# Four transformer blocks with cross-attention on one core: TensorE's steps woven in pairs, and GpSimd waiting inside each stack

## The chip, the core and the metric

The kernel runs on one NeuronCore of a Trainium2 chip. The engines are TensorE (PE: matmuls and their weight loads, PEld), VectorE (DVE), ScalarE (ACT), GpSimd (POOL) and SyncE (SP, which here issues DMAs). The metric is the device time of one launch in microseconds (us).

## The reference, cut to what matters

A batch of 4 sequences, 256 tokens by 128 features, goes through four blocks. With `heads` splitting 128 features into 16 heads of 8:

```python
def attend(q, k, v):
    w = softmax(einsum('bhqd,bhkd->bhqk', heads(q), heads(k)) / sqrt(8))
    return einsum('bhqk,bhkd->bhqd', w, heads(v))
...
x = x + gate * (attend(q, k, v of modulate(ln(x))) @ W + b)
x = x + attend(q of ln(x), k, v of ln(context)) @ W + b
x = x + gate * mlp(modulate(ln(x)))
```

Blocks 0 and 1 are self-attention, cross-attention and a GELU MLP; block 2 is one cross-attention with modulated norms; block 3 is a self-attention in shifted windows of 64 tokens, a cross-attention in which each query keeps only its 16 highest scores per head, and a SwiGLU MLP. That makes seven attentions (l = 0 to 6; l = 5 is "window", l = 6 is "topk", the others "full") and three MLPs (l = 7, 8, 9), in the order 0, 1, 7, 2, 3, 8, 4, 5, 6, 9 for each of the 4 batches.

## The kernel before

**Steps and their order.** The work is cut into steps (kind, batch b, layer l, number u). Each engine runs its own fixed list, `ORDERS[engine]`, worked out before the launch by `plan` (line 623). `plan` is a list scheduler: it places the ready step with the highest rank first. A rank is the length of the tail of work behind the step plus priorities from tables (`LEAD`, `BIAS`, `EXTRA`). `BUSY` holds the planner's durations, `SLOTS` the buffers: 8 PSUM banks, 2 slots of key and query parts, 3 of weights. The four batches are independent chains, and the lists interleave them. At run time engines wait for semaphores, each in its own order.

**One attention.** VectorE takes mean and variance (`stats`), GpSimd centres x (`z`: lines 1168 to 1172, the first of which negates the mean), TensorE transposes it (`normed`, L1505), ScalarE copies it with the modulation. TensorE projects keys and queries (L1517, L1518). ScalarE and GpSimd split them into high and low parts (`k_parts`, `qk`; L1278, L1281, L1187). GpSimd then issues four DMAs (`stack`, u = 0 to 3, L1158), each of which lays one plane of 4 heads into `qk_stack`, 32 partitions for each head. A plane is 256 KB. Nothing but these DMAs goes through GpSimd's DMA queue.

**Scores and weights.** A step of `scores` or `weights` (u = 0 to 7) covers two heads of plane u // 2, in row groups 0 and 1 of TensorE where u is even and 2 and 3 where it is odd. For the full kind it is four matmuls with 32 rows and 256 columns, two tiles of 128 queries by two heads, into two banks:

```python
for t in range(NT):
    for j in range(2):
        g = 2 * (u % 2) + j
        ins = nc.tensor.matmul(ps[:, j, at:at + (P if window else N)], ...
```

VectorE reduces the scores to row maxima (L1406). TensorE transposes these (L1554), ScalarE copies them, and SyncE lays them into the stack by an 8 KB DMA (`maxima`, L1120, "qk_stack<-centred" in the trace). Then the `weights` steps repeat the product transposed (L1566), ScalarE takes the exponential (L1298), and `mix` multiplies by the values (L1590). The topk layer has 16 steps of one head each (L1544). For each one VectorE runs two passes that find the 16 highest (L1416 to L1429), and GpSimd turns the rest into a mask (L1227), which TensorE adds (L1577).

**What the planner assumes.** A step of scores or weights costs TensorE 0.46 us, and 0.22 less right behind a step in the other row groups (`beside`). A `stack` step costs GpSimd 1.0 us. Its data move 1.9 us later, or when the queue is free, for 1.25 us. A row DMA lands 2.2 us after its issue, whatever else is in flight. Where TensorE is expected to stand idle, spare matmuls on the identity are put in (L1473).

**Start.** GpSimd waits for the key rows (`k_rows_s`, line 1151) ahead of its whole list. They are a constant of the stack that ScalarE's queue loads.

Of the kernel before, what the change touches and what calls it, by code (L numbers as in the profile page):

```python
# [141 lines left out]
def scores_of(l):  # L142
# [8 lines left out]
    ("dve", "stats"): 0.68, ("pool", "z"): 2.0, ("pe", "normed"): 0.36, ("act", "normed"): 0.45,  # L151
    ("pe", "qk"): 1.0, ("act", "k_parts"): 0.94, ("act", "qk"): 0.95, ("pool", "k_parts"): 0.77, ("pool", "qk"): 0.77, ("sp", "load"): 0.6, ("pool", "stack"): 1.0,
# [22 lines left out]
TO_QUEUE, STACK_TIME, LANDS, AHEAD = 1.9, 1.25, 0.6, 1.75  # L175
HOP = 0.13
SLOTS = {"bank": 8, "qk": 2, "pt": 3, "picks": 2, "gd": 2}
# [12 lines left out]
    ("act", "context", 0, 1): -13.2, ("act", "context", 0, 2): 4.2, ("act", "context", 0, 6): -9.8,  # L190
    ("act", "context", 0, 8): -1.0, ("act", "context", 0, 9): -3.6, ("act", "context", 1, 0): -5.2,
    ("act", "context", 1, 1): -13.1, ("act", "context", 1, 5): -0.7, ("act", "context", 1, 8): 0.1,
    ("act", "context", 2, 0): -40.0, ("act", "context", 2, 1): 7.3, ("act", "context", 2, 3): -4.9,
    ("act", "context", 2, 4): -13.1, ("act", "context", 2, 5): -8.1, ("act", "context", 2, 7): 4.4,
    ("act", "context", 2, 8): -0.9, ("act", "context", 2, 9): -6.1, ("act", "context", 3, 1): 2.2,
    ("act", "context", 3, 2): 19.7, ("act", "context", 3, 3): -3.5, ("act", "context", 3, 5): -26.8,
    ("act", "context", 3, 6): 0.1, ("act", "context", 3, 7): -100.0, ("act", "context", 3, 9): 66.2,
    ("act", "heads_out", 0, 0): 0.9, ("act", "heads_out", 0, 2): 53.8, ("act", "heads_out", 0, 3): -12.5,
    ("act", "heads_out", 0, 4): -4.9, ("act", "heads_out", 0, 6): -4.8, ("act", "heads_out", 0, 7): -24.5,
    ("act", "heads_out", 0, 9): 28.8, ("act", "heads_out", 1, 3): -14.3, ("act", "heads_out", 1, 4): 3.5,  # L200
    ("act", "heads_out", 1, 5): -3.0, ("act", "heads_out", 1, 9): 34.0, ("act", "heads_out", 2, 1): 1.7,
    ("act", "heads_out", 2, 2): 50.5, ("act", "heads_out", 2, 4): 11.8, ("act", "heads_out", 2, 5): 5.1,
    ("act", "heads_out", 2, 6): 0.9, ("act", "heads_out", 2, 7): -3.6, ("act", "heads_out", 2, 8): -21.0,
    ("act", "heads_out", 2, 9): -0.2, ("act", "heads_out", 3, 1): -17.5, ("act", "heads_out", 3, 2): 58.0,
    ("act", "heads_out", 3, 3): -12.8, ("act", "heads_out", 3, 5): 3.4, ("act", "heads_out", 3, 6): -8.5,
    ("act", "heads_out", 3, 8): 0.9, ("act", "heads_out", 3, 9): -42.0, ("act", "k_parts", 0, 2): 66.7,
    ("act", "k_parts", 0, 4): 1.2, ("act", "k_parts", 0, 5): -29.6, ("act", "k_parts", 0, 7): -7.7,
    ("act", "k_parts", 0, 9): 35.2, ("act", "k_parts", 1, 0): 16.0, ("act", "k_parts", 1, 3): 56.6,
    ("act", "k_parts", 1, 4): -12.3, ("act", "k_parts", 1, 5): 1.0, ("act", "k_parts", 1, 7): 4.9,
# [358 lines left out]
    ("pe", "values"): 0.1, ("pool", "gated"): 0.6, ("pool", "k_parts"): -3.6, ("pool", "pre"): -11.2,  # L568
    ("pool", "qk"): 137.4, ("pool", "stack"): -3.6, ("pool", "topk"): 283.6, ("pool", "z"): -2.3,
    ("sp", "load"): -114.6, ("sp", "maxima"): 115.5, ("sp", "store"): 42.9,  # L570
}


def w_group(blk):
# [48 lines left out]
def plan(lead, landed, table_load=1.3, patience=0.0):  # L623
# [222 lines left out]
    while left:  # L846
# [25 lines left out]
        if beside(t, s):  # L872
            d, lag = d - 0.22, 0.2
# [799 lines left out]
```

## Time and profile before

| | us |
|---|---|
| median of 3 runs | 672.29 |
| lowest and highest | 669.69, 678.34 |
| the profiled execution | 665.29 |
| its span, first to last instruction | 663.5 |
| mean granted clock of TensorE | 0.863 |

In the profiled execution PE is busy 570.0 us (86% of the span), DVE 490.9 (74%), ACT 386.3 (58%), POOL 306.4 (46%). A busy time says how long an engine had an instruction in it, not that it set the pace: that is read from the windows and the waits. In rows of lines, "L12" is line 12 of the kernel, the text is output<-inputs, x is the count, and behind the bar stand busy us and mean ns, then the idle time ahead of the instructions and who ended it. Granted clock 1.0 is full speed.

### The profile page before, as it was taken

Reading aid. Unit: us, or ns where it says so; the run is one execution under the profiler, and the core shown is the slowest. Engines: PE = TensorE matmul, PEld = TensorE weight load, DVE = VectorE, ACT = ScalarE, POOL = GpSimd, SP = SyncE. Lnnn points to the kernel's source line nnn. Section 1 sums busy time; section 2 is a strip of 40 time slices with the busy share of each in tenths; the row PEclk is TensorE's granted clock in tenths of the full one; section 3 lists DMA queues with packets and bytes.
Section 4 is the critical chain, followed back from the end, with each engine's and each line's share of the span. In section 5 each row is a group of like instructions: output and inputs, shape, how many; then the busy total and the mean of one; then the engine's idle time right before and its main releaser. Section 6 shows DMA issues by size and latency. Waiting matters only on the chain.

```text
span 663.5 us, 14489 instructions
## 1 busy us (share of the span) xinstructions
PE 570.0 (86%) x5152; PEld 378.9 (57%) x5152; DVE 490.9 (74%) x1291; ACT 386.3 (58%) x669; POOL 306.4 (46%) x584
## 2 busy tenths in 40 slices
PE   3888989899999999999998889786999987867477
PEld 3645556566756565657665556554655664634246
DVE  2577767853859687745377727999999999999953
ACT  2546878799696887886757766452233531611133
POOL 6884535435845444364562446641341446111133
PEclk9858999999999999998989979777575795765779
DMA  9560344302333533020335043140020002000000
GB/s 319 143 159 3 88 106 112 73 2 54 76 67 69 105 77 78 2 65 2 66 72 123 2 129 68 28 101 0 2 65 2 2 10 64 9 1 2 1 2 16
DMA packets 15062, 39.23 MB, mean 59 GB/s; under 512 B 2641, under 2 KB 6801, under 8 KB 14737
## 3 DMA queue, kind: packets, MB, share of 16 engines
q0 software_dynamic: 8960, 29.37, 20.1%
q1 hardware_dynamic: 5312, 8.46, 3.8%
q8 instruction: 43, 0.70, 0.4%
q10 hardware_dynamic: 720, 0.49, 0.3%
q14 instruction: 27, 0.21, 0.1%
HBM read 7.96 MB, written 0.52 MB: 13 GB/s over the span
## 4 chain that ended last, share of the span: by engine, by line
DVE 38%; PE 37%; ACT 8%; DMA 6%; issue 6%; POOL 4%; ACTq 0%; POOLq 0%
PE psum L1590 10%; DVE left L1419 8%; DVE left L1429 7%; DVE top L1426 6%; DVE top L1416 6%; DVE maxima L1406 5%; PE psum L1566 5%; PE psum L1536 5%; ACT softmax_T L1298 4%; DMA qk_stack<-centred 3%; PE psum L1625 3%; PE psum L1636 3%; DMA qk_stack<-qk_parts 2%; DVE maxima L1402 2%; PE psum L1617 2%
## 5 line engine op out<-in xcount | busy, mean ns | idle before, releaser
L1298 ACT ACTIVATE softmax_T<-psum 128x1024 f32<-128x1024 f32 (+1 forms) x224 | 210.9, 962 | 111.7 <-PE psum L1577 73.3
L1406 DVE TENSOR_REDUCE maxima<-psum 128x4 f32<-128x1024 f32 x160 | 190.1, 1216 | 52.4 <-PE psum L1536 51.6
L1566 PE MATMUL psum<-qk_stack 32*128 32x256 f32 (+1 forms) x896 | 114.9, 346 | 28.1 <-DMA qk_stack<-centred 9.6
L1590 PE MATMUL psum<-softmax_T,values 128*32 128x256 f32 (+1 forms) x1792 | 129.9, 408 | 4.8 <-ACT softmax_T L1298 3.5
L1566 PEld LDWEIGHTS psum<-qk_stack 32*128 32x128 f32 x896 | 72.3, 202 | 71.0 <-issue 31.0
L1227 POOL TENSOR_SCALAR unpicked<-left 128x512 bf16<-128x512 f32 x64 | 39.5, 616 | 136.0 <-DVE left L1429 135.3
L1536 PE MATMUL psum<-qk_stack 32*128 32x256 f32 (+1 forms) x768 | 89.6, 335 | 9.2 <-ACT softmax_T L1298 2.4
L1536 PEld LDWEIGHTS psum<-qk_stack 32*128 32x128 f32 x768 | 58.9, 200 | 37.5 <-issue 16.5
L1590 PEld LDWEIGHTS psum<-softmax_T,values 128*32 128x32 f32 x1792 | 56.7, 118 | 40.3 <-issue 12.0
L1187 POOL TENSOR_TENSOR qk_parts<-qk_parts 128x256 fp32r<-128x256 f32 x56 | 40.9, 730 | 77.0 <-ACT qk_parts L1281 76.6
L1158 POOL DMA_DIRECT2D qk_stack<-qk_parts x112 | 63.7, 580 | 7.0 <-POOL qk_parts L1187 6.3
L1306 ACT ACTIVATE centred<-psum 8x256 f32<-8x256 f32 (+1 forms) x64 | 23.1, 364 | 56.3 <-PE psum L1551 40.9
L1278 ACT ACTIVATE qk_parts<-psum,column_biases 128x512 fp32r<-128x512 f32 x56 | 38.5, 687 | 24.0 <-PE psum L1518 21.0
L1419 DVE MATCH_REPLACE8 left<-top,psum 128x256 f32<-128x256 f32 x128 | 52.0, 414 | 0.0
L1429 DVE MATCH_REPLACE8 left<-top,left 128x256 f32<-128x256 f32 x128 | 51.4, 408 | 0.0
L1416 DVE MAX8 top<-psum 128x8 f32<-128x256 f32 x128 | 48.1, 417 | 2.0 <-PE psum L1544 2.0
L1426 DVE MAX8 top<-left 128x8 f32<-128x256 f32 x128 | 47.9, 416 | 1.3
L1448 DVE TENSOR_TENSOR x<-x,psum 128x256 f32<-128x256 f32 x40 | 16.6, 414 | 41.2 <-PE psum L1636 22.9
L1473 PE MATMUL psum<-identity 128*128 128x256 bf16 x150 | 27.4, 332 | 19.4 <-DVE left L1419 11.5
L1310 ACT ACTIVATE mixed_T<-psum 128x256 f32<-128x256 f32 x56 | 21.5, 385 | 31.9 <-PE psum L1590 31.3
L1172 POOL TENSOR_SCALAR centred<-x,neg_mean,rstd 128x128 f32<-128x128 f32 x80 | 35.2, 447 | 4.4
L1168 POOL TENSOR_SCALAR neg_mean<-mean_var 128x2 f32<-128x2 f32 x48 | 9.4, 196 | 58.6 <-DVE mean_var L1394 44.1
(99 smaller groups left out, 870.3 us busy)
## 6 DMA issues: line engine op xcount, KB each, us to landing
qk_stack<-qk_parts POOLq DMA_DIRECT2D x112, 256.0 KB, 5.1
weights<-in_w SPq DMA_DIRECT2D x1, 1408.0 KB, 13.5
row_biases<-in_rows SPq DMA_DIRECT2D x1, 1088.0 KB, 10.8
weights<-in_w SPq DMA_DIRECT2D x2, 512.0 KB, 5.9
weights<-in_w SPq DMA_DIRECT2D x1, 832.0 KB, 9.0
qk_stack<-centred SPq DMA_DIRECT2D x48, 8.0 KB
weights<-in_w SPq DMA_DIRECT2D x1, 768.0 KB, 4.3
weights<-in_w SPq DMA_DIRECT2D x1, 576.0 KB, 3.7
```

The lines of the kernel that those rows point to most:

```text
L1158: pool.dma_start(QKS[b][:, u, :, :].bitcast(F32), parts[32 * u:32 * u + 32, slot, :, :, :].bitcast(F32)).then_inc(stacked[b][u], 16)
L1187: nc.gpsimd.tensor_tensor(lo, lo.bitcast(F32), parts[:, slot, 0, c, :].bitcast(F32), ALU.subtract).then_inc(done[kind, "pool"], 1)
L1227: nc.gpsimd.tensor_scalar(unpicked[:, n, :, :], left[:, k, :, :], 1.0 / GONE, 1.0, ALU.mult, ALU.add).then_inc(done[kind, "pool"], 1)
L1298: nc.scalar.activation(pT[:, slot, u % 2, :, 0:cols].rearrange("p (i t) n -> p i t n", t=NT), two_banks(step).rearrange("p i (t n) -> p i ...
L1406: nc.vector.tensor_reduce(rows[:, u // 4, u // 2 % 2, g:g + 2, :], ps.rearrange("p i (t k) -> p i t k", t=NT), AX_X, ALU.max).then_inc(fin, 1)
L1416: ins = nc.vector.max(top8[:, b, r, g, t, :], misc[:, N * t:N * t + N])
L1419: ins = nc.vector.match_replace(left[:, k, t, :], top8[:, b, r, g, t, :], misc[:, N * t:N * t + N], -GONE)
L1426: ins = nc.vector.max(top8[:, b, 2, g, t, :], left[:, k, t, :])
L1429: ins = nc.vector.match_replace(left[:, k, t, :], top8[:, b, 2, g, t, :], left[:, k, t, :], -GONE)
L1536: ins = nc.tensor.matmul(ps[:, j, at:at + (P if window else N)], QKS[b][32 * g:32 * g + 32, s, 0, P * t:P * t + P], QKS[b][32 * g:32 * g + ...
L1566: ins = nc.tensor.matmul(ps[:, i, t, 0:P if window else N], QKS[b][32 * g:32 * g + 32, s, 1, P * t:P * t + P], QKS[b][32 * g:32 * g + 32, ...
L1590: ins = nc.tensor.matmul(misc[32 * g:32 * g + 32, queries], V[:, b, t, first:first + 32], pT[:, slot, g // 2, 2 * (g % 2) + t, 0:P if wind ...
```

## The change

It has five parts. TensorE's list may hold woven pairs: two steps of scores, weights (but not those of topk) or topk whose row groups differ. Both sets of waits come first, and then the first tile of A, the first of B, the second of A and the second of B are issued. The planner forms a pair where the second step can start within 0.15 us of the first, and prices it at 0.44 us. `BUSY` has 1.9 for `z` and 0.62 for `stack` in place of 2.0 and 1.0, row DMAs are priced by what is in the queue ahead of them, the scores and weights of odd u need no longer follow those of the even u before, x and context are assumed to land 0.8 and 1.2 us later, and `EXTRA`, `BIAS` and `LEAD` hold other numbers throughout, so all orders differ. GpSimd waits for the key rows only ahead of the first stack. The negated mean is dropped; the mean is subtracted in place. And GpSimd issues plane 2 of a stack only when plane 0 has landed, and plane 3 only when plane 1 has; the planner has no term for this wait.

```diff
-    ("dve", "stats"): 0.68, ("pool", "z"): 2.0, ("pe", "normed"): 0.36, ("act", "normed"): 0.45,
+    ("dve", "stats"): 0.68, ("pool", "z"): 1.9, ("pe", "normed"): 0.36, ("act", "normed"): 0.45,
...
+ROWS_WAY, ROWS_BEHIND = 1.5, 3.0
...
+WOVEN, WOVEN_BESIDE, WOVEN_FIRST, WOVEN_SECOND, WOVEN_SLOWER, TOGETHER = 0.44, 0.1, 0.42, 0.43, 1.67, 0.15
...
+def weaves(step):
+
+    kind, b, l, u = step
+    if kind == "topk":
+        return True
+    return kind == "scores" and ATTN[l]["kind"] == "full" or kind == "weights" and ATTN[l]["kind"] != "topk"
...
-                t = task("pe", ("weights", b, l, u), maxed[u // 2], prev and ("pe", ("weights", b, l, u - 1)),
+                t = task("pe", ("weights", b, l, u), maxed[u // 2], ("pe", ("weights", b, l, u - 1)) if u and (u % 2 == 0 or topk) else None,
...
+        if eng == "pe" and weaves(step):
+            others = [(rank(n), c[0], n) for n in ready["pe"] if (c := choose(n)) is not None]
+            fit = [o for o in others if weaves(o[2][1]) and not groups(o[2]) & groups(t) and o[1] <= s + TOGETHER]
+            if fit:
+                r, at, other = max(fit, key=lambda o: o[0])
+                if any(r + BESIDE < o[0] for o in others if o not in fit and o[1] <= s + 0.3):
+                    other = None
...
+        if other is not None:
+            s = max(s, at)
+            d = WOVEN - (WOVEN_BESIDE if beside(t, s) else 0.0)
...
+            woven[step] = other[1]
...
-            land = end + TO_QUEUE + 0.3
...
+            land = end + ROWS_WAY + min(max(0.0, queue - end - 0.64), ROWS_BEHIND)
...
+ORDERS, SLOT, HAD, TIMES, SPARE, WOVEN_WITH = plan(LEAD, landed)
...
-            pool.wait_ge(k_rows_s, 16 * SLOTS["qk"])
+            first_stack = next(i for i, s in enumerate(ORDERS["pool"]) if s[0] == "stack")
             for step in ORDERS["pool"]:
                 kind, b, l, u = step
                 if kind == "stack":
                     slot = SLOT["qk", ("k_parts", b, l, 0)][0]
+                    if step == ORDERS["pool"][first_stack]:
+                        pool.wait_ge(k_rows_s, 16 * SLOTS["qk"])
+                    if u > 1:
+                        pool.wait_ge(stacked[b][u - 2], 16 * (l + 1))
...
-                    nc.gpsimd.tensor_scalar(nmean[:, b, c, :], mv[:, b, c, :, 0], -1.0, 0.0, ALU.mult, ALU.add)
...
-                        ins = nc.gpsimd.tensor_scalar(dst[:, b, t, :], src[:, b, t, :], nmean[:, b, c, t:t + 1],
-                                                      rstd[:, b, c, t:t + 1], ALU.add, ALU.mult)
+                        ins = nc.gpsimd.tensor_scalar(dst[:, b, t, :], src[:, b, t, :], mv[:, b, c, t, 0:1],
+                                                      rstd[:, b, c, t:t + 1], ALU.subtract, ALU.mult)
...
+            def half(step, t):
...
+                s, ps = u // 2, two_banks(step)
+                own, other = (1, 0) if kind == "weights" else (0, 1)
+                moving = slice(P * t, P * t + P) if ATTN[l]["kind"] == "window" else slice(0, N)
+                for j in range(2):
+                    g = 2 * (u % 2) + j
+                    ins = nc.tensor.matmul(ps[:, j, t * N:t * N + moving.stop - moving.start],
+                                           QKS[b][32 * g:32 * g + 32, s, own, P * t:P * t + P],
+                                           QKS[b][32 * g:32 * g + 32, s, other, moving], start=True, stop=True)
+                return ins
...
+                if weaves(step):
+                    inputs_in(step)
+                    if step in WOVEN_WITH:
+                        other = WOVEN_WITH[step]
+                        banks_free(pe, other)
+                        inputs_in(other)
+                        half(step, 0)
+                        half(other, 0)
+                        half(step, 1).then_inc(fin, 1)
+                        half(other, 1).then_inc(done[other[0], "pe"], 1)
+                    else:
+                        half(step, 0)
+                        half(step, 1).then_inc(fin, 1)
```

## Rows read from the trace of the kernel before

**Rows 1.** The page, busy tenths in 40 slices of 16.6 us.

```profile
PE   3888989899999999999998889786999987867477
DVE  2577767853859687745377727999999999999953
```

**Rows 2.** Windows: length, busy us (count) of PE, PEld, DVE, ACT, POOL, then clock.

```profile
20.00:60.00 40.00, 33.51 (x251) 20.89 (x250) 27.65 (x46) 18.82 (x38) 29.33 (x59) 0.66 0.49 120
60.00:400.00 340.00, 317.38 (x3286) 209.28 (x3288) 223.27 (x362) 266.15 (x452) 171.00 (x330) 0.97 0.30 67
400.00:640.00 240.00, 191.25 (x1458) 126.81 (x1459) 227.25 (x839) 85.83 (x151) 83.72 (x149) 0.72 0.11 25
```

**Rows 3.** Groups of lines, 400 to 640 us: busy us, mean ns, idle before.

```profile
L1419 DVE MATCH_REPLACE8 left<-top,psum 128x256 f32<-128x256 f32 x128 | 52.0, 414 | 0.0
...
L1426 DVE MAX8 top<-left 128x8 f32<-128x256 f32 x128 | 47.9, 416 | 1.3
```

**Rows 4.** Timeline of PE: start us, length us; two places.

```profile
101.95 0.50 PE L1566 MATMUL psum<-qk_stack 32*128 32x256 f32 x4
102.38 0.44 PE L1505 MATMUL psum<-identity,context_centred 128*128 128x128 f32 x2
...
106.44 0.39 PE L1566 MATMUL psum<-qk_stack 32*128 32x256 f32 x2
106.48 0.39 PE L1536 MATMUL psum<-qk_stack 32*128 32x256 f32 x2
106.67 0.28 PE L1566 MATMUL psum<-qk_stack 32*128 32x256 f32 x2
106.68 0.30 PE L1536 MATMUL psum<-qk_stack 32*128 32x256 f32 x2
```

**Rows 5.** Windows of the tile qk_stack alone, PE first.

```profile
60.00:400.00 340.00, 118.12 (x1258) 76.81 (x1260) 42.92 (x76) 0.97 0.30 67
```

**Rows 6.** Groups of lines, 60 to 400 us, DVE and ACT.

```profile
L1406 DVE TENSOR_REDUCE maxima<-psum 128x4 f32<-128x1024 f32 x141 | 167.9, 1216 | 43.2 <-PE psum L1536 42.4
L1298 ACT ACTIVATE softmax_T<-psum 128x1024 f32<-128x1024 f32 (+1 forms) x159 | 155.3, 1001 | 20.7 <-PE psum L1566 19.1
```

**Rows 7.** Timeline of DVE and of POOL in the first 10 us.

```profile
6.67 0.25 DVE L1394 BATCH_NORM_AGGREGATE mean_var<-stats 128x2 f32<-128x6 f32 x2
...
9.48 0.19 POOL L1168 TENSOR_SCALAR neg_mean<-mean_var 128x2 f32<-128x2 f32 x1 [3.07 <-DMA qk_parts<-in_k_rows]
```

**Rows 8.** Groups of lines of POOL, whole span.

```profile
L1158 POOL DMA_DIRECT2D qk_stack<-qk_parts x112 | 63.7, 580 | 7.0 <-POOL qk_parts L1187 6.3 <-issue 0.4
L1168 POOL TENSOR_SCALAR neg_mean<-mean_var 128x2 f32<-128x2 f32 x48 | 9.4, 196 | 58.6 <-DVE mean_var L1394 44.1 <-PE psum L1505 11.1 <-DMA qk_parts<-in_k_rows 3.1
```

**Rows 9.** The chain of work near 80 us, and the list of waits.

```profile
79.96 4.84 DMA qk_stack<-centred
...
PE psum L1566 <- DMA qk_stack<-centred: 9.6, 9, 2.2
PE psum L1505 <- POOL centred L1172: 4.6, 6, 1.6
```

**Rows 10.** Timeline of POOL from 214 us, and of PE at 220 us.

```profile
214.18 2.25 POOL L1158 DMA_DIRECT2D qk_stack<-qk_parts  x4
216.41 0.25 POOL L1168 TENSOR_SCALAR neg_mean<-mean_var 128x2 f32<-128x2 f32 x1
217.84 0.88 POOL L1172 TENSOR_SCALAR centred<-x,neg_mean,rstd 128x128 f32<-128x128 f32 x2
...
220.40 0.44 PE L1505 MATMUL psum<-identity,centred 128*128 128x128 f32 x2 [0.28 <-DVE maxima L1406]
```

**Rows 11.** DMA issues, median us to landing, around 160.2, 156.1 and 215.8 us.

```profile
qk_stack<-qk_parts POOLq DMA_DIRECT2D x1, 256.0 KB, 3.4
...
qk_stack<-qk_parts POOLq DMA_DIRECT2D x2, 256.0 KB, 4.0
...
qk_stack<-qk_parts POOLq DMA_DIRECT2D x2, 256.0 KB, 5.9
```

More of the change, by code:

```diff
@@ L195 @@
[L195 to L204, printed above, removed]
@@ L782, in plan @@
     lists = {e: [] for e in engines}
-    clock, spare = Clock(), {}
+    clock, spare, woven = Clock(), {}, {}
     table, last, queue = "exp", 0, 16.0
@@ L843, in choose, with hold, landing @@
         return s, taken
+    def hold(t, taken):
+        for ring, which in taken:
+            slots[ring] = [o for o in slots[ring] if o not in which]
+            slot[ring, t[1]] = [k for _, k, _ in which]
+            had[ring, t[1]] = sorted({before for _, _, before in which if before is not None})
+    def landing(t, land, end):
+        for r, taker in gives(t):
+            slots[r] += [(land + HOP, k, taker) for k in slot[r, taker]]
+            slots[r].sort()
+        for n in users[t]:
+            waiting[n] -= 1
+            ready_at[n] = max(ready_at[n], land + (HOP if n[0] != t[0] or land > end else 0.02))
+            if not waiting[n]:
+                ready[n[0]].append(n)
     left = len(order)
@@ L880, in plan @@
                 table = fn
-        if eng == "pe" and taken:
-            since = max([free["pe"], IDENTITY_THERE] + [when for _, which in taken for when, _, _ in which])
-            if s - since >= IDLE:
-                clock.until(since)
-                spare[step] = int(min(0.85 * (s - since), 0.3 + 0.6 * (s - since)) * (1.0 if clock.rate == 1 else 1 / 1.8) / SPARE_D)
-                if spare[step]:
-                    clock.run(since, spare[step] * SPARE_D, spare[step] * SPARE_CELLS, 1.8)
         end = clock.run(s, d, cells(step), SLOWER.get(kind, 1.8)) if eng == "pe" else s + d
@@ L891, in plan @@
         lists[eng].append(step)
-        for ring, which in taken:
-            slots[ring] = [o for o in slots[ring] if o not in which]
-            slot[ring, step] = [k for _, k, _ in which]
-            had[ring, step] = sorted({before for _, _, before in which if before is not None})
         land = end + lag
@@ new lines, in _ @@
+                    pe.wait_ge(consts_s, 3)
+                    for i in range(2):
+                        after(pe, "pool", ("topk", b, l, 2 * u + i))
+                        for t in range(NT):
+                            for r in range(NT):
+                                ins = nc.tensor.matmul(ps[:, i, t, P * r:P * r + P],
+                                                       unpicked[:, 4 * SLOT["picks", ("topk", b, l, 4 * s)][0] + 2 * (u % 2) + i, r, P * t:P * t + P], drop[:],
+                                                       start=False, stop=(t == 1 and r == 1))
```

526 lines of the change are left out of this document (276 added, 250 removed), and 339 rows, old and new, of tables (EXTRA, LEAD).

## Prediction

> **What bounds the kernel now.** I read the 40 slices of the page first, then the same span in a few windows. The slices [rows 1] show two stages. From slice 4 to slice 24 TensorE stands at 8 or 9 tenths and VectorE at 5 to 8; from slice 25 on VectorE stands at 9 and TensorE falls. The windows [rows 2] put numbers on that. From 60 to 400 us TensorE is busy 317.4 of 340 us (93%), ScalarE 266.2 (78%), VectorE 223.3 (66%), GpSimd 171.0 (50%), at a clock of 0.97. From 400 to 640 us VectorE is busy 227.3 of 240 us (95%), TensorE 191.3 with a clock of 0.72. The groups of lines name VectorE's work there: four lines of the top-16 passes, 128 instructions each, between 47.9 and 52.0 us a line [rows 3], some 200 us together. None of it falls in the first stage, so the kernel is TensorE's for 340 us and then VectorE's for 240 us, and a microsecond saved in the first stage arrives whole only if the second stage starts earlier by it. The start, 20 to 60 us, is a third case: TensorE at 33.5 of 40 us with a clock of 0.66, GpSimd at 29.3 of 40 (73%) [rows 2].
>
> The diff does five things: it weaves pairs of steps on TensorE, it lets the planner know of that (and gives it other priorities), it lets GpSimd begin before the key rows have landed, it drops one small GpSimd instruction of each norm, and it makes GpSimd wait in the middle of each stack.
>
> **1. Weaving.** A lone step of scores or weights is four matmuls, two row groups by two tiles. It starts at 101.95 and the next step starts at 102.38 [rows 4]: 0.43 us. The change issues the first tile of A, the first tile of B, the second of A, the second of B. What does the kernel before do when two such steps stand next to each other? The four rows at 106.44 [rows 4] answer: two matmuls of L1566, two of L1536, two of L1566, two of L1536, starts 106.44, 106.48, 106.67, 106.68, the last one over at 106.98. The program has all of L1566's step ahead of L1536's, and yet the trace shows them woven already, at 0.54 us for both where a lone one takes 0.50. So for a pair that is adjacent and ready the new program order gives nothing: my value is 0 for these. What can give is the planner: it now prices a pair at 0.44 us in place of about 0.70, and so puts more steps side by side.
>
> The Trainium skill ("TensorE: Matmul & The Clock Gate", section The mechanism) says that matmuls of different row groups start and end in strict program order, without reordering. By that rule a pair in the kernel before would run end to end, and weaving in the program would save the second switch of weights in each. The rows at 106.44 differ from it, and the measurement decides; what it would give is one of the rivals below.
>
> How much can more pairs give? From 60 to 400 us the matmuls that read the stack keep TensorE busy 118.1 us, 1258 of them [rows 5], which is 315 steps of four at 0.375 us each (some are paired now). If every step were half of a pair at 0.43 us for two, that would be 315 x 0.215 = 68 us, so 50 us less; if no further pair forms, 0. Those are the bounds: -50 and 0. Between them I go by the readers. A pair takes four of the eight banks, and the readers need 1.216 us on VectorE and 1.001 us on ScalarE for each step [rows 6], two to three times what TensorE needs to fill it. ScalarE is already at 266 of 340 us, and every shortening pushes it up: at 50 us less it would stand at 266 of 290 (92%). Four free banks at one time, with both inputs landed within 0.15 us of each other, is not the common case. I take a quarter of the room, -13 us. The second stage adds nothing: its matmuls of this kind lie beside a VectorE that is 95% busy.
>
> The Trainium skill ("TensorEngine Tiling (Array Packing)", section PSUM Bottleneck) states that tiling speeds up TensorE but not the emptying of PSUM, which can become the bottleneck. The two rows of the readers agree with it, and it is why I stay far from the upper bound.
>
> **2. The start.** GpSimd's first instruction of the first norm starts at 9.48 after 3.07 us of waiting for the key rows [rows 7]; nothing of the norm reads them. The wait moves to the first stack, at 20 us, when they are long there. Mean and variance of the first batch are there at 6.92 [rows 7], 2.5 us before that norm starts, all four first norms follow one another on GpSimd, and the first stack follows them, so I take -2.5 us (bounds -3.1 and 0; next late would be the weights of the first projection).
>
> **3. The dropped negation.** L1168, 48 instructions of 196 ns, 9.4 us of GpSimd [rows 8]. It lies on the way from statistics to the norm's transpose, but TensorE waits for the centred tile only 4.6 us in the whole span [rows 9]. So 48 x 0.2 us is the upper bound of the gain, 4.6 is the one that waits show, and I take -2. The subtraction in place of an addition keeps the operation's shape, and I give it no other price.
>
> **4. The wait inside a stack.** Today the four planes are issued in a row, 2.25 us [rows 10], 112 issues at 580 ns [rows 8]. A plane with nothing ahead of it lands 3.4 us after its issue, two in a row 4.0 (the median of both), the last two of four 5.9 [rows 11]. With the change plane 2 is issued when plane 0 has landed: some 3.6 us after the first issue, where it was 1.1. It then has little ahead of it and lands at about 3.6 + 3.6 = 7.2 instead of 1.1 + 5.9 = 7.0. Plane 3 waits for plane 1, which lands at about 0.6 + 4.3 = 4.9, and lands at about 4.9 + 3.6 = 8.5 instead of 1.7 + 5.9 = 7.6. (3.6 and 4.3 are my estimates around the 3.4 and 4.0 of the rows.) For the planes themselves I take 0: plane 2 is first read by the fifth step of its attention, four reductions of 1.216 us [rows 6] after the first.
>
> The price is GpSimd's. It is in order, and a stack holds it until plane 3 is out: 4.9 + 0.6 = 5.5 us instead of 2.25, 3.2 us more, 28 times, some 90 us on an engine that is busy 284 us between 20 and 640 us [rows 2]. Queued behind the waiting instruction is whatever GpSimd has next: the norm of another batch, the low parts of its keys and queries, the gated weights, the unpicked masks. TensorE waits for these. The case at 214.18 [rows 10] shows how far the cover goes: the stack ends at 216.43, the norm of another batch starts at 216.41, its centred tile is over at 218.72, and TensorE transposes it at 220.40. It has 1.7 us in hand. 3.2 us later it would be 1.5 us late, and TensorE, in order too, would stand still. That is the upper bound if every stack had such a follower with such a cover: 28 x 1.5 = 42 us; the lower bound is 0, since GpSimd is idle half of the time and a follower may come later. The planner prices a plane at 0.62 us and does not know of the wait, so nothing in the order makes room. I take a quarter, +10 us, because the other three quarters find an idle GpSimd or a slack of more than 3 us.
>
> **5. The row DMAs.** The wait also takes something off: the 8 KB transfer of the maxima runs behind stacks, and in the chain one of them takes 4.84 us [rows 9]. TensorE waits 9.6 us in nine places for it [rows 9]. With at most two planes in flight, and with a planner that prices the queue, I take -3 (bounds -9.6 and 0).
>
> **The sum.** Against the profiled execution, 665.3 us with its 663.5 us span: 665.3 - 13 - 2.5 - 2 - 3 + 10 = 654.8. The median of the runs shown is 672.3, 7.0 above the profiled one, and I carry that over: **661.8 us**, 1.6% less than before. About 2% is what a measurement of this kernel tells from no change.
>
> **The rivals.**
> (a) *The planner finds far more pairs and the wait is hidden.* For it: TensorE is idle only 23 of 340 us, so whatever pairs save there is time, and VectorE has 117 us to spare in that stage. Against it: the readers and the eight banks. With -35 for the pairs and +2 for the wait: 665.3 - 35 - 2.5 - 2 - 3 + 2 = 624.8, and 632 as a median.
> (b) *GpSimd becomes the engine that paces.* The place is the first 60 us and every norm behind a stack. At the start GpSimd is at 29.3 of 40 us [rows 2]; four stacks stand there, and 4 x 3.2 = 12.8 us more is more than the 10.7 us that it has free (40 - 29.3), so the first layers of the later batches slip. If half of the 42 us of point 4 reach TensorE and pairs give 0: 665.3 - 2.5 + 21 = 683.8, 691 as a median. It decides from the point where the wait costs more than the other four give, here 20.5 us; it is slower by 2% when it costs 13 us more than that.
> (c) *Neither works.* Adjacent steps are woven already, no further ones form, the wait falls into GpSimd's idle time: 665.3 - 2.5 = 662.8, 670 as a median.
> (d) *The program's order does what the engine does not.* If most pairs ran end to end today, each would save one switch, 0.215 us; 157 pairs in the first stage make 34 us. That gives 665.3 - 34 - 2.5 - 2 - 3 + 10 = 633.8, 641 as a median. The rows at 106.44 speak against it; I leave it 3%.
>
> **How the numbers follow.** My forecast 40%, (a) 20%, (b) 20%, (c) 17%, (d) 3%. The forecast itself spreads by about 12 us either way, from the quarters that I chose in points 1 and 4. The edge of faster by 2% is at 658.8 and that of slower at 685.7. Faster: (a), (d) and some 15 of the 40 points of the forecast, 0.38. Slower: (b) and a point of the rest, 0.21. Within: 0.41. The range goes from 638, which leaves out half of (a), to 690, which leaves out half of (b).
>
> **What would show it.** Weaving: on TensorE's timeline more groups of eight matmuls of the two lines inside 0.55 us, and from 60 to 400 us fewer busy microseconds for the matmuls of the stack at the same count. If only pairs of the old kind are there, step 1 was wrong. The start: the first negation's place taken by the variance line at about 7 us and the first stack at about 17. The wait: GpSimd's rows of L1158 (at its new line) in groups of two with a gap of 2 to 3 us, the new releaser a plane's DMA, and TensorE's waits for the centred tile and ScalarE's for its key parts. If TensorE's waits for these stay near 5 us, the wait is hidden. The rows: no 8 KB transfer of more than 3 us in the chain. The topk stage would keep its 200 us of VectorE and only begin earlier. What would make me wrong is the order itself: both programs run a fixed order from a planner, and a different set of priorities may place one batch's top-16 work earlier beside TensorE's stage, for which no row of before gives a price.

## The result: 10% slower

| | before | after |
|---|---|---|
| median us | 671.1 | 738.1 |
| lowest and highest | 669.7, 678.3 | 732.9, 744.9 |
| span of the profiled execution | 663.5 | 743.1 |
| mean granted clock of TensorE | 0.863 | 0.814 |

The ratio is 1.101, with a 95% interval of 1.095 to 1.108. The forecast was 661.8 us and its range ended at 690. The executions of one kernel fall into a faster and a slower group; every ratio below compares faster ones alone, every median takes all of them, and the profiled execution of the changed kernel, 6.8 us above its median, is one of the slower ones.

The page of the changed kernel, in the form of [rows 1]; a slice is now 18.6 us:

```profile
PE   4568888799778897889788699659979869787867
...
DVE  2375836673356667473655444668999999999953
```

The windows of [rows 2] again, with one more, because the end is 80 us later:

```profile
20.00:60.00 40.00, 24.54 (x178) 16.25 (x176) 23.25 (x40) 12.40 (x28) 25.89 (x44) 0.66 0.54 120
60.00:400.00 340.00, 290.86 (x2785) 186.76 (x2789) 193.07 (x312) 231.37 (x383) 162.03 (x256) 0.89 0.25 52
400.00:640.00 240.00, 194.74 (x1635) 127.88 (x1627) 190.71 (x619) 103.41 (x197) 99.85 (x166) 0.71 0.21 44
640.00:743.00 103.00, 79.14 (x585) 56.24 (x584) 79.96 (x300) 29.39 (x44) 27.63 (x43) 0.84 0.02 5
```

No engine is full from 60 to 400 us any more. TensorE was busy 317.4 us there with 3286 matmuls [rows 2] and is now busy 290.9 with 2785. ScalarE and VectorE lose 35 and 30 us with it, GpSimd 9. The granted clock of the stage fell too, from 0.97 to 0.89, while TensorE stood idle for 49 us of it and not 23: 64 matmuls of one line (L1625, now L1708) took 394 ns each before and 460 now. What the clock adds to the loss was not told apart. So an engine waits, and the others wait for it. The list of waits names it (engine, waiting line, releaser: us in total, times, longest):

```profile
DVE maxima L1462 <- PE psum L1543: 112.2, 61, 7.9
POOL qk_stack L1215 <- DMA qk_stack<-qk_parts: 99.2, 50, 4.4
...
PE psum L1604 <- POOL centred L1228: 43.5, 27, 4.5
...
PE psum L1604 <- POOL context_centred L1228: 12.6, 3, 7.2
```

GpSimd waits 99.2 us for planes to land, 3.5 us in each of 28 stacks; this wait did not exist before. TensorE waited 4.6 us for centred tiles [rows 9]; it now waits 56.1 us for the two kinds. VectorE's waits for TensorE (112.2 us, and 51.6 before) are the same loss once more, one engine on. One case, on the timeline of GpSimd and then of TensorE (start, length, and in brackets the idle time ahead):

```profile
87.85 1.18 POOL L1215 DMA_DIRECT2D qk_stack<-qk_parts  x2 [0.30 <-POOL qk_parts L1243]
91.73 0.55 POOL L1215 DMA_DIRECT2D qk_stack<-qk_parts  x1 [2.70 <-DMA qk_stack<-qk_parts]
92.90 0.55 POOL L1215 DMA_DIRECT2D qk_stack<-qk_parts  x1 [0.62 <-DMA qk_stack<-qk_parts]
93.52 0.19 POOL L1225 TENSOR_SCALAR var_eps<-mean_var 128x2 f32<-128x2 f32 x1
93.80 0.71 POOL L1226 TENSOR_TENSOR rstd<-var_eps,half_power 128x2 f32<-128x2 f32 x1
94.61 1.58 POOL L1228 TENSOR_SCALAR centred<-x,mean_var,rstd 128x128 f32<-128x128 f32 x2
```

```profile
96.33 0.66 PE L1604 MATMUL psum<-identity,centred 128*128 128x128 f32 x2 [2.03 <-POOL centred L1228]
```

Planes 2 and 3 go out 3.9 and 5.1 us after the first (forecast 3.6 and 4.9). Behind them on the in-order GpSimd stands the norm of another batch, and TensorE stands still 2.03 us for it. Of those 2.03 us, 1.58 - 0.88 = 0.7 come from the norm's last row itself, which took 0.88 us for two tiles before [rows 10]; the dropped negation gives 0.2 of them back. The chain of waits shows the same stretch (start, length, what):

```profile
88.48 4.13 DMA qk_stack<-qk_parts
...
92.90 0.55 POOL qk_stack L1215
...
94.61 1.59 POOL centred L1228 x2
...
96.33 0.66 PE psum L1604 x2
```

The groups of lines of GpSimd give both causes their totals (x count, busy us, mean ns, idle before):

```profile
L1215 POOL DMA_DIRECT2D qk_stack<-qk_parts x112 | 63.6, 568 | 105.9 <-DMA qk_stack<-qk_parts 99.2 <-POOL qk_parts L1243 6.6
L1228 POOL TENSOR_SCALAR centred<-x,mean_var,rstd 128x128 f32<-128x128 f32 x80 | 63.2, 797 | 4.2
```

A centred tile costs 797 ns with the mean subtracted. The added form costs 447 to 454 ns in every kernel below that has it.

### The profile page after: what moved, and what is told of

The parts are those of the page before. It is cut to its first block, busy times and chain, and to the rows that moved or that the text cites. A ratio compares the mean times of both kernels' runs of the same rounds, so it can differ in the third digit from the quotient of the medians.

```text
span 743.1 us, 14558 instructions
## 1 busy us (share of the span) xinstructions
PE 599.1 (81%) x5218; PEld 394.8 (53%) x5218; DVE 491.9 (66%) x1291; ACT 384.6 (52%) x667; POOL 331.4 (45%) x534
## 4 chain that ended last, share of the span: by engine, by line
PE 29%; DVE 23%; POOL 18%; issue 14%; DMA 10%; ACT 5%; POOLq 0%; ACTq 0%; DVEq 0%
DMA qk_stack<-qk_parts 10%; PE psum L1673 7%; POOL centred L1228 5%; PE psum L1543 5%; DVE left L1475 5%; DVE left L1485 5%; DVE top L1482 4%; DVE top L1472 4%; POOL qk_parts L1243 3%; POOL rstd L1226 3%; PE psum L1708 3%; POOL qk_stack L1215 3%; DVE maxima L1462 3%; ACT softmax_T L1354 2%; PE psum L1719 2%
## 5 line engine op out<-in xcount | busy, mean ns | idle before, releaser
L1462 DVE TENSOR_REDUCE maxima<-psum 128x4 f32<-128x1024 f32 x160 | 189.6, 1216 | 112.6 <-PE psum L1543 112.2
L1543 PE MATMUL psum<-qk_stack 32*128 32x256 f32 (+1 forms) x1408 | 137.4, 361 | 17.6 <-ACT softmax_T L1354 9.1
L1673 PE MATMUL psum<-softmax_T,values 128*32 128x256 f32 (+1 forms) x1792 | 138.3, 431 | 5.3 <-ACT softmax_T L1354 4.0
L1543 PEld LDWEIGHTS psum<-qk_stack 32*128 32x128 f32 x1408 | 90.9, 214 | 78.0 <-issue 33.7
L1215 POOL DMA_DIRECT2D qk_stack<-qk_parts x112 | 63.6, 568 | 105.9 <-DMA qk_stack<-qk_parts 99.2
L1673 PEld LDWEIGHTS psum<-softmax_T,values 128*32 128x32 f32 x1792 | 59.5, 124 | 44.8 <-issue 20.0
L1243 POOL TENSOR_TENSOR qk_parts<-qk_parts 128x256 fp32r<-128x256 f32 x56 | 40.7, 729 | 95.2 <-ACT qk_parts L1337 94.9
L1228 POOL TENSOR_SCALAR centred<-x,mean_var,rstd 128x128 f32<-128x128 f32 x80 | 63.2, 797 | 4.2
L1604 PE MATMUL psum<-identity,centred 128*128 128x128 f32 x80 | 19.9, 340 | 44.4 <-POOL centred L1228 43.5
L1559 PE MATMUL psum<-identity 128*128 128x256 bf16 x216 | 37.0, 317 | 12.4 <-DVE cond_silu L1402 6.2
L1504 DVE TENSOR_TENSOR x<-x,psum 128x256 f32<-128x256 f32 x40 | 16.6, 416 | 43.3 <-PE psum L1700 24.2
L1491 DVE RECIPROCAL rden<-psum 128x32 f32<-128x32 f32 x28 | 9.9, 353 | 44.8 <-PE psum L1682 44.7
L1604 PEld LDWEIGHTS psum<-identity,centred 128*128 128x128 f32 x80 | 9.5, 163 | 53.9 <-issue 39.0
```

Source lines behind the costliest of these rows:

```text
L1215: pool.dma_start(QKS[b][:, u, :, :].bitcast(F32), parts[32 * u:32 * u + 32, slot, :, :, :].bitcast(F32)).then_inc(stacked[b][u], 16)
L1228: ins = nc.gpsimd.tensor_scalar(dst[:, b, t, :], src[:, b, t, :], mv[:, b, c, t, 0:1], rstd[:, b, c, t:t + 1], ALU.subtract, ALU.mult)
L1243: nc.gpsimd.tensor_tensor(lo, lo.bitcast(F32), parts[:, slot, 0, c, :].bitcast(F32), ALU.subtract).then_inc(done[kind, "pool"], 1)
L1462: nc.vector.tensor_reduce(rows[:, u // 4, u // 2 % 2, g:g + 2, :], ps.rearrange("p i (t k) -> p i t k", t=NT), AX_X, ALU.max).then_inc(fin, 1)
L1543: ins = nc.tensor.matmul(ps[:, j, t * N:t * N + moving.stop - moving.start], QKS[b][32 * g:32 * g + 32, s, own, P * t:P * t + P], QKS[b][3 ...
L1673: ins = nc.tensor.matmul(misc[32 * g:32 * g + 32, queries], V[:, b, t, first:first + 32], pT[:, slot, g // 2, 2 * (g % 2) + t, 0:P if wind ...
```

## The experiments

The first theory was: the wait costs what its hold of GpSimd costs, and the dropped negation is a loss because the subtraction is slower. Rivals: the new orders are bad by themselves; or the planes are late, and not GpSimd. "The order before" means the old planner numbers, "the new order" the changed ones. Ratios are to the kernel before, run beside, with 95% intervals.

### The parts, one at a time

The wait, alone in the kernel before:

```diff
+                    if u > 1:
+                        pool.wait_ge(stacked[b][u - 2], 16 * (l + 1))
```

> The kernel before with the two waits inside each stack, order and norm of before. Theory H: 671 rises by 25 us or more. My recorded sum gave +10, the half of its upper bound +21. If it rises by 10 or less, the hold costs only in the new order, whose planner prices a plane at 0.62 us in place of 1.0.

> The changed kernel without the two waits inside a stack; all else as changed. Theory H (the hold of GpSimd is the cost: 99 us of waiting on planes in 50 places, with norms and key parts queued behind it): 735 falls by 40 to 65 us, to 670 to 695. Theory N (the norm's subtraction with a column of mean_var is the cost: 797 ns in place of 447, 96 times, 34 us): it falls by less than 25 us. Theory O (the order and the woven pairs are worse by themselves): it stays above 700 whatever is taken away.

The subtraction, alone in the kernel before, and taken back out of the changed one (the reverse of this diff):

```diff
-                    nc.gpsimd.tensor_scalar(nmean[:, b, c, :], mv[:, b, c, :, 0], -1.0, 0.0, ALU.mult, ALU.add)
...
-                        ins = nc.gpsimd.tensor_scalar(dst[:, b, t, :], src[:, b, t, :], nmean[:, b, c, t:t + 1],
-                                                      rstd[:, b, c, t:t + 1], ALU.add, ALU.mult)
+                        ins = nc.gpsimd.tensor_scalar(dst[:, b, t, :], src[:, b, t, :], mv[:, b, c, t, 0:1],
+                                                      rstd[:, b, c, t:t + 1], ALU.subtract, ALU.mult)
```

> The kernel before with the new norm alone (no negation, mean subtracted from mean_var). Each norm on GpSimd gets 0.2 us shorter by the negation and 0.7 longer by two centring instructions at 797 ns. Theory N: 671 rises by 10 us or more. If centring stays at 447 ns here and the time falls by 0 to 3 us, the slow form needs something else of the changed kernel.

> The changed kernel with the norm of before (negated mean in its own tile, added) and with the waits. Theory N: 735 falls by 20 to 34 us, to 701 to 715. Theory H: it falls by 10 us or less. Theory O: it falls by 10 us or less. In each case the centring instructions return to 447 ns if it is their form that makes them slow.

Both parts, in the kernel before; and neither, in the changed one:

> The kernel before with both the waits and the new norm. If the two costs simply add, its rise is the sum of the rises of the two kernels that hold one each; if both draw on the same slack (GpSimd's idle time and the norm's cover of about 1 us), it is more than the sum. If the order is no cause, this kernel reaches the 735 of the changed one within 10 us.

> The changed kernel without the waits and with the norm of before: the new order, the woven pairs and the early start alone. H and N together: 650 to 668, at or a little under before (671), since the pairs form and the start is 2.5 us earlier. Theory O: above 685.

Measured, in us (median; ratio with its interval):

| | order before | new order |
|---|---|---|
| neither | 671.1 (1) | 666.6 (0.993, 0.989 to 0.998) |
| subtraction | 679.9 (1.010, 0.991 to 1.029) | 684.1 (1.022, 1.012 to 1.032) |
| wait | 701.9 (1.048, 1.042 to 1.055) | 719.0 (1.074, 1.066 to 1.082) |
| both | 715.4 (1.067, 1.052 to 1.082) | 738.1 (1.101, 1.095 to 1.108) |

So the new order by itself is not the loss: without the two GpSimd parts it is 0.7% faster than the kernel before. In it the wait costs 719.0 - 666.6 = 52 us and the subtraction 17.5; together that is 70, and both measured 71.5. In the order before the wait costs 31 us and the subtraction 7 us by its ratio, 9 by the medians (its interval reaches below 0). TensorE's waits for centred tiles follow. They stand here for the order before with the wait, for the new order with the wait, then for the new order with neither:

```profile
POOL qk_stack L1160 <- DMA qk_stack<-qk_parts: 97.4, 45, 4.1
...
PE psum L1507 <- POOL centred L1174: 14.9, 14, 3.1
...
PE psum L1538 <- DMA qk_stack<-qk_parts: 10.4, 4, 4.1
...
PE psum L1568 <- DMA qk_stack<-centred: 3.5, 6, 0.8
```

```profile
PE psum L1606 <- POOL centred L1230: 28.1, 16, 4.2
...
PE psum L1606 <- POOL context_centred L1230: 10.4, 3, 6.9
```

```profile
PE psum L1604 <- POOL centred L1228: 3.1, 6, 1.0
...
PE psum L1653 <- DMA qk_stack<-centred: 1.0, 3, 0.4
```

The hold is as long in either order (97.4 and 98.6 us of waiting); what differs is how much of it reaches TensorE: 17.4 us of waits for centred tiles of both kinds in the order before (2.5 of them for the context's) and 38.5 in the new one. The difference, 21 us, is as large as that of the two prices. In the order before TensorE also waits 10.4 us for planes themselves, in four places, all in the window attention; in the kernel before it was 2.0.

### Is it the operation or the place of its operand?

The changed line differs in two things: it subtracts, and it reads the mean from the strided tile of statistics. The first kernel copies the mean, not negated, to its own tile and subtracts it; the second negates it where it is and adds it:

```diff
-                    nc.gpsimd.tensor_scalar(nmean[:, b, c, :], mv[:, b, c, :, 0], -1.0, 0.0, ALU.mult, ALU.add)
+                    nc.gpsimd.tensor_scalar(nmean[:, b, c, :], mv[:, b, c, :, 0], 1.0, 0.0, ALU.mult, ALU.add)
...
-                                                      rstd[:, b, c, t:t + 1], ALU.add, ALU.mult)
+                                                      rstd[:, b, c, t:t + 1], ALU.subtract, ALU.mult)
```

> The kernel before with the mean copied unnegated to its own tile and subtracted there: tells the operation from the operand's place. If the subtraction makes centring slow, its line stands at 797 ns here; if the column of mean_var does, at 447. Time: 671 to 674 at 447 ns, like the new norm plus 0.2 us each at 797.

```diff
-                    nc.gpsimd.tensor_scalar(nmean[:, b, c, :], mv[:, b, c, :, 0], -1.0, 0.0, ALU.mult, ALU.add)
+                    nc.gpsimd.tensor_scalar(mv[:, b, c, :, 0], mv[:, b, c, :, 0], -1.0, 0.0, ALU.mult, ALU.add)
...
-                        ins = nc.gpsimd.tensor_scalar(dst[:, b, t, :], src[:, b, t, :], nmean[:, b, c, t:t + 1],
+                        ins = nc.gpsimd.tensor_scalar(dst[:, b, t, :], src[:, b, t, :], mv[:, b, c, t, 0:1],
```

> The kernel before with the mean negated in place in mean_var and added from there: the other half of the same question. If the place makes centring slow, 797 ns here; if the subtraction does, 447 ns and a time like before.

The second one changes the computation in one place: the two norms of a batch's context share their statistics, so the later one meets a mean that was negated twice. The amount of work is the same. Subtracting from its own tile, and then adding from the statistics (groups of lines):

```profile
L1172 POOL TENSOR_SCALAR centred<-x,neg_mean,rstd 128x128 f32<-128x128 f32 x80 | 63.2, 795 | 4.4
```

```profile
L1171 POOL TENSOR_SCALAR centred<-x,mean_var,rstd 128x128 f32<-128x128 f32 x80 | 35.2, 447 | 4.4
```

It is the operation. The place costs nothing in the instruction's own time. The times go with it: 679.0 us (1.018, 1.001 to 1.036, two runs) and 669.4 (1.004, 0.997 to 1.011).

### GpSimd's time or late planes?

The wait does two things: it holds GpSimd, and it lets planes 2 and 3 land later. One pair of kernels holds GpSimd with the planes on time, by clears of a scratch tile behind every fourth plane (7 or 12 clears, linked one to the next):

```diff
+                    n_planes[0] += 1
+                    if n_planes[0] % 4 == 0:
+                        for _ in range(12):
+                            link(nc.gpsimd.memset(scratch[:], 0.0))
```

> The kernel before without any wait on planes, but with seven linked clears of a scratch tile (about 0.45 us each, 3.2 us) on GpSimd behind each fourth plane. The planes are issued and land as before; only GpSimd is taken for as long as by the hold. Theory Q (the price is GpSimd's queue: norms and key parts stand behind it): +25 to +35 us, as with the waits (+31). Theory L (the price is that planes 2 and 3 land later): +5 us or less.

> As the run with seven clears, which measured 0.26 us a clear with its link and so took GpSimd for only 1.85 us a stack (+11), but with twelve of them, 3.2 us, the length of the hold. Planes are issued and land as before. Theory Q (GpSimd's queue is the price): +22 to +35 us. Theory L (planes 2 and 3 late): it stays at +11 or below +15.

> The new order with the old norm and no wait (666.6 us), with 12 clears of a scratch tile on GpSimd behind every fourth plane, about 3.2 us per stack, planes on time. In the old order the same clears cost +27 us and the wait +31. If the wait's price is GpSimd's time and the new order has less slack on GpSimd, the clears cost more here: +40 to +52 us, 707 to 719 us. If the extra 21 us of the new order come from the late planes (the planner has their readers earlier), the clears cost about +27 us as before, 694 us.

The other kernels let the planes be late with GpSimd free: SyncE issues planes 2 and 3, with the same wait or, as its own comparison, without it:

```diff
+                if kind == "stack":
+                    slot = SLOT["qk", ("k_parts", b, l, 0)][0]
+                    sp.wait_ge(stacked[b][u - 2], 16 * (l + 1))
...
+                if kind == "stack" and u > 1:
+                    continue
```

> The kernel before with planes 2 and 3 issued by SyncE, each with the same wait for the plane two places ahead; GpSimd issues only planes 0 and 1 and waits for none. Planes land as late as in the kernel with the waits. Theory Q: within 8 us of before, or below it, since GpSimd gets 1.1 us a stack back. Theory L: +20 us or more. A price of its own: the rows of the maxima stand behind the waiting plane on SyncE, up to 3.6 us, in the places where a stack and a row meet.

> As the gated one on SyncE, without the waits on planes. GpSimd is freed of 56 issues, 32 us, and nothing is late. Theory Q: -2 to -10 us against before. Theory L: 0 (nothing is later than before).

> The new order with the norm of before, no wait on planes, and planes 2 and 3 issued by SyncE. The new order without the waits stands at 0.993 of before. Theory Q: 0.975 to 0.99. If SyncE's rows suffer behind 256 KB planes, 1.0 or above.

> The new order with the old norm, planes 2 and 3 issued by SyncE with the same wait, GpSimd free; without the wait the same kernel took 672.2 us. If the late planes cost nothing by themselves: 672 to 678 us. If they make up the new order's extra price: about 21 us more, 690 us and above.

| | order before | new order |
|---|---|---|
| 7 clears a stack | 681.5 | |
| 12 clears a stack | 700.0 | 700.1 (1.057, 1.045 to 1.068) |
| planes by SyncE, no wait | 668.7 (1.001, 0.994 to 1.007) | 672.2 (1.003, 0.998 to 1.007) |
| planes by SyncE, wait | 674.9 (1.004, 0.998 to 1.009) | 671.9 (1.012, 1.005 to 1.020) |

The runs of the two kernels without a ratio lie too far apart for one (665.4 to 686.6, and 687.5 to 706.2); beside them before had medians of 670.7 and 672.9. The lowest run of each had a granted clock of 0.858 and 0.851, and beside runs of before at nearly that clock, 668 and 669 us, they make nothing for 7 clears (665.4) and 19 us for 12 (687.5). So by the two ways of reading it 7 clears cost between nothing and 11 us, and 12 clears 19 to 27. The 12 clears in the order before, in groups and in waits:

```profile
L1165 POOL MEMSET scratch<- 128x128 f32 x336 | 70.0, 208 | 17.8
```

```profile
PE psum L1511 <- POOL centred L1178: 17.6, 13, 3.1
```

The clears take (70.0 + 17.8) / 28 = 3.1 us a stack, near the hold's 3.5, and with every plane on time they cost 19 to 27 us where the wait costs 31; TensorE's waits for centred tiles are 17.6 us, with the wait 14.9. With late planes and a free GpSimd these waits are 4.0 us, those for planes 0.7, and the time is above its comparison by 6 us in the one order and not at all in the other (by the ratios 2 and 7 us). So most of the price is that of GpSimd's queue. Whether it grows in proportion to the time held, 51.2 us with 7 clears and 87.8 with 12, can't be told from these runs.

The new order pays more for the same clears: 700.1 - 666.6 = 34 us (by the ratios 6.4%, or 43 us). That is not all of its 52. I expected 707 to 719 us had it been, and 694 had the order made no difference; 700.1 lies between. Late planes alone don't make up the rest (671.9 beside 672.2; by the ratios 1%, with intervals that touch). Between 4 and 18 us of the wait in the new order stay open. They too arrive as late norms: TensorE waits 38.5 us for centred tiles of both kinds with the wait and 27.3 with the clears.

### Is it the start?

Rival (b) laid the loss first on the 20 to 60 us window. The wait only for the first layer, and the key rows' wait alone moved to the first stack:

```diff
+                    if u > 1 and l == 0:
+                        pool.wait_ge(stacked[b][u - 2], 16 * (l + 1))
```

> The kernel before with the waits in the first layer's four stacks only, 4 of 28. If the price is per stack, 31 x 4/28 = 4 us. If it sits at the start, where GpSimd is 73% busy and four stacks follow one another, as my rival (b) put it, 10 us or more.

```diff
-            pool.wait_ge(k_rows_s, 16 * SLOTS["qk"])
...
+                    if step == ORDERS["pool"][first_stack]:
+                        pool.wait_ge(k_rows_s, 16 * SLOTS["qk"])
```

> The kernel before with the wait for the key rows moved ahead of the first stack, nothing else. My recorded term is -2.5 us. If weights or another arrival take its place, 0; GpSimd's first norm then starts near 7 us all the same.

The wait in the first layer alone costs nothing: 670.4 us (1.001, 0.997 to 1.004), with 11.6 us of waiting in six places. The moved wait gives 670.9 us (0.996, 0.992 to 1.001): the first norm starts at 7.62 us instead of 9.48 [rows 7] and the first stack at 18.67 instead of 19.97. That can't be told from no gain.

The wait in the first layer alone was run in the order before only, and the traces show that the new order is different there. Its list for GpSimd has the first norm of a context right behind the second stack, and its list for TensorE has the transpose early: at 27.93 us without the wait, where the kernel before has it at 34.60. With the wait (the new order, the norm of before) it comes at 32.67, after the longest wait of the whole kernel for a centred tile:

```profile
32.67 0.66 PE L1606 MATMUL psum<-identity,context_centred 128*128 128x128 f32 x2 [6.90 <-POOL context_centred L1230]
```

The window of 20 to 60 us, first of the new order with neither part and then with the wait, in the form of [rows 2]:

```profile
20.00:60.00 40.00, 34.74 (x265) 22.32 (x263) 29.15 (x50) 19.41 (x37) 32.86 (x71) 0.66 0.46 117
```

```profile
20.00:60.00 40.00, 26.19 (x191) 17.20 (x193) 24.52 (x42) 14.59 (x30) 26.59 (x55) 0.65 0.51 117
```

TensorE has 8.6 us less of its work done there; in the order before the wait takes 0.8 (33.5 to 32.7). So about 8 of the 21 us by which the new order pays more for the wait lie at the start, if none of them is made up later.

### Does the program's order of a pair matter?

The new order without wait and subtraction, its pairs issued one step after the other:

```diff
                         half(step, 0)
-                        half(other, 0)
                         half(step, 1).then_inc(fin, 1)
+                        half(other, 0)
                         half(other, 1).then_inc(done[other[0], "pe"], 1)
```

> The new order without the waits and with the norm of before, and each of the 69 pairs issued as the kernel before issues two neighbours: all four matmuls of A, then all four of B (both sets of waits still first). Theory R (the engine or its queue weaves neighbours of different row groups by itself, as the rows at 106.44 suggest): the same time as with woven issue, 0.993 of before within 0.5%, and pairs of lines still alternate in the trace. Theory P (program order counts): 69 pairs at 0.2 us, up to 14 us more, 1.01 or above.

665.8 us (0.993, 0.989 to 0.997), and woven 666.6 (0.993). A pair in TensorE's timeline of the unwoven kernel:

```profile
106.49 0.51 PE L1543 MATMUL psum<-qk_stack 32*128 32x256 f32 x8
```

Eight matmuls in 0.51 us, with the program's order A, A, B, B; both steps have one line here, so the rows show the time of a pair and not who alternates. The matmuls of the stack alone, from 60 to 400 us, first of the woven and then of the unwoven kernel, in the form of [rows 5]:

```profile
60.00:400.00 340.00, 108.85 (x1198) 70.67 (x1200) 40.74 (x72) 0.94 0.28 63
```

```profile
60.00:400.00 340.00, 110.65 (x1240) 71.29 (x1241) 43.00 (x76) 0.97 0.29 65
```

Per step of four that is 0.363 and 0.357 us; before it was 0.375 [rows 5]. The clock was 0.94, 0.97 and 0.97, so it is the last two that compare.

## Why the prediction was wrong

**Where it failed.** Two terms of the sum. The main one is point 4: "I take a quarter, +10 us, because the other three quarters find an idle GpSimd or a slack of more than 3 us". Measured it is +31 us in the order before, three quarters of my upper bound of 42, and +52 in the new one, above the bound. The working up to there held: 3.2 us a stack, some 90 us, stand against 99.2 measured; the queue behind it and the waiting engine were named rightly. What failed is how much of it arrives, and the trace of before could have told. Its 48 norms can be followed by the lists, from the end of the centred tile on GpSimd to the start of its transpose on TensorE: 36 of the 48 have less than 3.2 us in hand, 29 less than 1.5, and the median is 1.1. Of the 24 that stand at most three places behind a plane in GpSimd's list, 19 have less than 3.2. So three quarters of the norms lack the slack that I gave to three quarters of the stacks. I judged the cover by an average (GpSimd idle half of the time), though the one case I had looked at showed 1.7 us in hand for 3.2 us of delay. GpSimd's idle time lies in waits for other engines' results, 94.9 us for ScalarE's key parts alone in the changed kernel. The bound itself was too low because it gave every late norm a cover of 1.7 us, and most have less. I also took 0 for the planes themselves, and in the order before TensorE waits 8 us more for them. The point where rival (b) decides, 20.5 us, was passed by this term alone.

The second is point 3: "The subtraction in place of an addition keeps the operation's shape, and I give it no other price". It takes 797 ns and not 447. For 96 tiles that is 34 us more of GpSimd against the 9.4 us of the dropped rows, and each norm ends 2 x 0.35 - 0.2 = 0.5 us later. Measured: +7 to +9 us in the order before, not clear of noise, and +17.5 in the new one, where I had -2. The trace of before has no tensor_scalar with a subtraction on GpSimd, so this price needed bounds from both sides, and I took a row of another operation for it.

**The sum again**, by what the runs gave: new orders with the start, -4; wait +52; subtraction +17.5; 671.1 + 65.5 = 736.6, beside 738.1 measured. Each term is a difference of measured kernels, so the sum says only that the parts nearly add.

**Point 1, weaving.** The value 0 for the program's order held: the unwoven kernel is as fast (0.993 and 0.993), and rival (d) is out. The starts at 106.44 [rows 4] have L1536 at 106.48, ahead of L1566's second tile at 106.67. That is not the strict program order of starts and ends that the Trainium skill states ("TensorE: Matmul & The Clock Gate", section The mechanism), and here the measurement decides. The -13 for more pairs did not come: all of the new order, start included, is -4 us. Per step of the stack it did save, 0.375 to 0.357 us at the same clock, or 6 us over 315 steps. The lists of TensorE say why it isn't more: of the kinds that may be woven, topk aside, 101 pairs of neighbouring steps in different row groups stand in the list before and 123 in the new one (69 of all its pairs are planned as woven). Two lone steps take 2 x 0.43 us and a pair 0.44 (106.49 to 106.93, where the next matmuls start) to 0.54, so 22 more pairs save 7 to 9 us, an estimate and at most if all are ready together. How much of the -4 is due to pairs and how much to the other planner numbers wasn't told apart.

**Point 2, the start.** -2.5 forecast, 0.4% (2.4 us) measured with an interval that includes 0. In the changed kernel nothing is left of it: the first norm starts at 6.93 us, but four norms later, each with the longer subtraction, the first stack stands at 20.05, as before (19.97). In the new order without the wait it is at 19.77 with the subtraction and at 17.82 with the norm of before, four times 0.5 us earlier. The two rows of the changed kernel in GpSimd's timeline are:

```profile
6.93 0.19 POOL L1225 TENSOR_SCALAR var_eps<-mean_var 128x2 f32<-128x2 f32 x1 [0.69 <-DVE mean_var L1450]
...
20.05 1.33 POOL L1215 DMA_DIRECT2D qk_stack<-qk_parts  x2 [0.65 <-POOL qk_parts L1243]
```

**Point 5, the rows.** The waits for row DMAs fell from 9.6 us [rows 9] to 3.5 with the wait in the order before, as the mechanism says. But they fall to 1.0 in the new order without any wait too. The gain exists and is small beside the rest.

**The rivals.** (b) was the right kind: GpSimd paces, and its place is "every norm behind a stack". Its other place, the first 60 us, was wrong for the order before, where the first layer's wait costs nothing, and right for the new one, where some 8 us of it lie. Its price, half of 42 us, was too low. (a) and (c) both have the wait hidden, which the first table excludes, and (d) falls with the unwoven kernel. The doubt that I named last, "the order itself", wasn't the cause by itself, but it set the price of the wait, 31 us or 52.

**The order's sensitivity.** The changed planner prices a plane at 0.62 us in place of 1.0. My reading is that this takes the slack out of GpSimd's order, 4 x 0.38 = 1.5 us a stack, that had absorbed part of a late norm before. The norms' cover agrees: its median is 1.1 us in the kernel before, and 0.8 and 0.4 in the new order's two kernels with neither part, woven and not. So do the clears (19 to 27 us in one order, 34 to 43 in the other). But all the other planner numbers changed as well, and a plan with only that price changed wasn't run: the link to that price is not shown.

## What to carry to other kernels

A wait that is put into an in-order queue costs what stands behind it: follow what is behind it to its readers, in all places and not in one, and compare the slack there with the hold; here three quarters of the norms had less than the hold, on an engine that was idle half of the time. If the landing of a transfer has to gate the next, put both on a queue with nothing urgent behind them: on SyncE the same wait costs 0 to 7 us, on GpSimd 31 to 52. And a change of an operation is a change of price until a row shows it, even where the shape stays and an instruction goes away.

## What the runs showed of the hardware

- On GpSimd, a tensor_scalar over 128x128 f32 with a per-partition operand took 794 to 799 ns as (subtract, multiply) and 447 to 454 as (add, multiply), in every kernel, wherever the operand lay.
- The eight matmuls of two neighbouring steps on different row groups took 0.51 us, whether the program had them A, B, A, B or A, A, B, B, and four alone 0.50 [rows 4].
- With planes issued only two at a time they landed 3.6 us after their issue (median), and 5.1 before; the total of a stack was still longer, since its issues took 5.6 us in the case at 87.85 and 2.25 before [rows 10].
